# Weighted sums of latents for four heads at a time in the second attention of a hybrid layer stack

## The reference, cut to what matters

```
ckv, k_pe = split(x @ wkv_a)             # 64 latents, 64 rotary
ckv = rmsnorm(ckv) * kv_norm_scale       # [256, 64], shared by all heads
k_nope, v = split(ckv @ wkv_b)           # per head
attn = softmax(causal(q k^T * scale))    # per head [256, 256]
out = concat_h(attn_h @ v_h) @ wo
```

## Time and profile before

| | us |
|---|---|
| median of 3 runs (1255.74 to 1257.43) | 1257.11 |
| the profiled execution | 1257.83 |
| its span, first to last instruction | 1256.0 |
| TensorE matmul busy over the span | 1025.7 (82%) |
| VectorE busy | 802.9 (64%) |
| ScalarE busy | 555.0 (44%) |
| GpSimd busy | 170.1 (14%) |
| TensorE busy from 648 to 1064 | 383.3 of 416.0 |
| VectorE busy there | 258.1 |
| ScalarE busy there | 231.4 |
| mean granted clock of TensorE there | 0.98 of full |

### The profile page before, as it was taken

How to read it: one execution, slowest core, us unless ns; L and a number is a source line. 1 busy time by engine, 2 the same in 40 slices (tenths; PEclk the granted TensorE clock), 3 DMA queues, 4 the chain that set the end, 5 groups by cost and what they waited for, 6 DMA issues and landing times.

```text
span 1256.0 us, 21238 instructions
## 1 busy us (share of the span) xinstructions
PE 1025.7 (82%) x7024; PEld 779.9 (62%) x7024; DVE 802.9 (64%) x2776; ACT 555.0 (44%) x1561; POOL 170.1 (14%) x188
## 2 busy tenths in 40 slices
PE   0477777877875899992879898898989898799998
PEld 0465555655643677761757777676777776677774
DVE  3346776777674888860356665656666665688883
ACT  1135344544451254551135554546555465144445
POOL 4212211221100011000011111110111100001101
PEclk9888888988886999996699999999999999699999
DMA  4442234412402323225000000000000000333331
GB/s 168 73 74 50 45 55 74 73 32 45 74 2 41 74 57 74 59 43 206 1 1 1 1 1 1 1 1 1 1 1 1 2 1 1 72 74 75 82 82 31
DMA packets 55003, 55.01 MB, mean 44 GB/s; under 512 B 4960, under 2 KB 53616, under 8 KB 54768
## 3 DMA queue, kind: packets, MB, share of 16 engines
q1 hardware_dynamic: 54896, 53.66, 20.7%
HBM read 35.29 MB, written 17.83 MB: 42 GB/s over the span
## 4 chain that ended last, share of the span: by engine, by line
PE 68%; DVE 17%; issue 6%; POOL 3%; ACT 3%; DMA 2%; SPq 1%; POOLq 0%; DVEq 0%; ACTq 0%
PE bank L288 20%; PE bank L1263 6%; PE bank L367 5%; PE bank L1551 5%; PE bank L1406 4%; PE bank L1539 4%; PE bank L1420 3%; PE bank L1403 3%; PE bank L1592 2%; PE bank L1390 2%; PE bank L1441 2%; DVE arena L889 2%; PE bank L346 2%; DVE arena L1057 1%; PE bank L1260 1%
## 5 line engine op out<-in xcount | busy, mean ns | idle before, releaser
L675 ACT ACTIVATE arena<-arena,neg_max 128x153 f32<-128x153 f32 x256 | 94.0, 417 | 148.3 <-DVE arena L889 146.4
L1057 DVE TENSOR_REDUCE arena<-bank 128x2 f32<-128x512 f32 (+1 forms) x192 | 129.6, 682 | 30.2 <-PE bank L1406 29.4
L754 ACT ACTIVATE weights<-bank 128x512 f32<-128x512 f32 x144 | 85.8, 597 | 110.0 <-PE bank L1420 109.7
L680 ACT ACTIVATE weights<-bank,neg_max 128x128 f32<-128x128 f32 (+1 forms) x256 | 105.2, 419 | 47.9 <-DVE neg_max L892 47.8
L378 ACT ACTIVATE weights<-bank 128x384 f32<-128x384 f32 (+1 forms) x184 | 83.4, 453 | 68.6 <-PE bank L367 68.2
L1406 PE MATMUL bank<-kf_stack,q_stack 96*128 96x128 f32 (+1 forms) x512 | 111.0, 321 | 0.0
L1263 PE MATMUL bank<-kbT,arena 128*128 128x128 f32 (+1 forms) x512 | 107.1, 333 | 0.0
L346 PE MATMUL bank<-cst,xn 128*128 128x128 f32 x128 | 26.3, 342 | 96.6 <-DVE xn L337 94.6
L1420 PE MATMUL bank<-q_stack,kf_stack 98*128 98x512 f32 x192 | 97.8, 513 | 0.0
L901 DVE TENSOR_SCALAR weights<-weights,inv_sum 128x128 f32<-128x128 f32 (+1 forms) x256 | 84.9, 374 | 4.6
L892 DVE TENSOR_REDUCE neg_max<-bank 128x1 f32<-128x128 f32 (+1 forms) x256 | 78.6, 349 | 9.9 <-PE bank L1263 8.3
(11 more groups left out here) (217 smaller groups left out, 2650.3 us busy)
## 6 DMA issues: line engine op xcount, KB each, us to landing
q_stack<-scr_q SPq DMA_DIRECT2D x96, 128.0 KB, 3.8
scr_q<-q_hi SPq DMA_DIRECT2D x24, 256.0 KB, 2.4
scr_q<-q_lo SPq DMA_DIRECT2D x24, 256.0 KB, 2.5
q_stack<-scr_q SPq DMA_DIRECT2D x24, 256.0 KB, 6.3
ka_stack<-scr_k SPq DMA_DIRECT2D x24, 192.0 KB, 5.0
x_all<-x SPq DMA_DIRECT2D x8, 256.0 KB, 9.0
arena<-b_wqn SPq DMA_DIRECT2D x1, 2048.0 KB, 8.0
arena<-b_wo SPq DMA_DIRECT2D x1, 2048.0 KB, 16.9
```

Of the source, the lines that this page charges most:

```text
L675: last = a.activation(pg[:, g % 2, t, j, 0:KA], s_guard[:, h % 2, t, 0:KA], ACT.Exp, scale=-1.0, bias=neg_max[:, h % 4, t:t + 1])
L680: last = a.activation(probs[:, h % 4, t * P:t * P + n], ps_s[h % 2][:, t * P:t * P + n], ACT.Exp, bias=neg_max[:, h % 4, t:t + 1], accum_o ...
L1057: v.tensor_reduce(into, p1[k % 2][:, :].rearrange("p (h k) -> p h k", h=n), AX.X, ALU.max, negate=True).then_inc(s["maxed"], 1)
```

## The change

Four heads form a group. `attend_b` runs for group `g` at `h` = 4, 8, 12 and after head 15. One matmul takes two heads side by side in its moving operand (heads `4g + j` and `4g + j + 2`), so it has 512 columns for the first keys and 256 for the last; again 4 matmuls, now for four heads, and they fill both column halves of the bank. `act_ctx` copies 128 by 512 elements once per group into all of `oT`; it waits for the projections of the group before. `project_b` is as it was for each pair, but starts at `h` = 5 instead of 3, and the last two pairs are projected after the loop. ScalarE's `copy_probs` waits for groups instead of pairs before it overwrites slots of `probsT`.

```diff
-                        if h % 2 == 0 and h:
-                            attend_b(b, par, h // 2 - 1)
-                        if h % 2 == 1 and h > 2:
-                            project_b(b, (h - 3) // 2)
+                        if h % G == 0 and h:
+                            attend_b(b, par, h // G - 1)
+                        if h % 2 == 1 and h > G:
+                            project_b(b, (h - G) // 2)
...
-            def act_ctx(b, p):
+            def act_ctx(b, g):
-                act.wait_ge(*at(sm, "o_ps", b, p + 1))
-                act.wait_ge(*at(sm, "wo_ps", b, p - 1))
-                a.activation(oT[:, p % 2, :], halves(ps_o)[:, p % 2, :], ACT.Copy).then_inc(sm["oT"], 1)
+                act.wait_ge(*at(sm, "o_ps", b, g + 1))
+                act.wait_ge(*at(sm, "wo_ps", b, 2 * g))
+                a.activation(oT[:, :, :], halves(ps_o), ACT.Copy).then_inc(sm["oT"], 1)
...
-                        if h % 2 == 0 and h > 0:
-                            act_ctx(b, h // 2 - 1)
+                        if h % G == 0 and h > 0:
+                            act_ctx(b, h // G - 1)
...
-            def attend_b(b, par, p):
-                pe_wait_copies(sm, b, 2 * p, 2)
-                pe.wait_ge(*at(sm, "oT", b, p))
+            def attend_b(b, par, g):
+                pe_wait_copies(sm, b, G * g, G)
+                pe.wait_ge(*at(sm, "oT", b, g))
                 for k, (lo, n) in enumerate(((0, T), (T, P))):
                     for j in range(2):
-                        last = mm(halves(ps_o)[j * LORA:(j + 1) * LORA, p % 2, T - n:T], kv_tok[par][:, k, 0:LORA],
-                                  probsT[:, (2 * p + j) % 8, lo:lo + n], start=k == 0, stop=k == 1,
-                                  skip_group_check=True)
+                        h = G * g % 8 + j
+                        last = mm(halves(ps_o)[j * LORA:(j + 1) * LORA, :, T - n:T], kv_tok[par][:, k, 0:LORA],
+                                  probsT[:, h:h + 3:2, lo:lo + n], start=k == 0, stop=k == 1, skip_group_check=True)
...
-                pe.wait_ge(*at(sm, "oT", b, p + 1))
+                pe.wait_ge(*at(sm, "oT", b, p // 2 + 1))
...
-                attend_b(b, par, H // 2 - 1)
-                project_b(b, H // 2 - 1)
+                attend_b(b, par, H // G - 1)
+                for p in range(H // 2 - 2, H // 2):
+                    project_b(b, p)
```

More of the change, by code:

```diff
@@ L158, in signals @@
             if kind != "f":
-                n_act, n_out = len(ON_ACT[kind]), 2 * H // G if kind == "b" else H // G
+                n_act, n_out = len(ON_ACT[kind]), H // G
                 per |= dict(scores=H, maxed=H, exp=H, pT_ps=H, copy_dve=H - n_act, copy_act=n_act, oT=n_out, o_ps=n_out)
@@ L693, in heads @@
                         late = s["kind"] == "a" and h in YT_SLOTS and not first
-                        copy_probs(act, s, b, h, n, 2 if s["kind"] == "b" else G,
+                        copy_probs(act, s, b, h, n, G,
                                    (lambda half: act_yT(b - 1, YT_SLOTS.index(h), half)) if late else None)
                     if s["kind"] == "b":
-                        if h % 2 == 0 and h > 0:
-                            act_ctx(b, h // 2 - 1)
+                        if h % G == 0 and h > 0:
+                            act_ctx(b, h // G - 1)
                     else:
@@ L830, in batch_b @@
                 heads(sm, b, par, first, left, 3 * P, step_b)
-                act_ctx(b, H // 2 - 1)
+                act_ctx(b, H // G - 1)
             run_batches(act, lambda: start(sm, step_b), batch_b)
```

## The result

The changed kernel takes 1262.5 us (median of 19 runs) against 1257.7 in the 19 runs of the kernel before beside it: ratio 1.0035, 95% interval 1.0019 to 1.0051. By the ratio that is 4.4 us slower, between 2.4 and 6.4 (the two medians lie 4.8 apart). The forecast was no change, 1257.6, range 1252 to 1262. Its direction and its range were both missed, the range by half a microsecond.

The account below looks back on a forecast made before the run. TensorE bounds the inside of a batch, latency its edge. Seven batches +0.5, last batch +1.9, disturbed batches -1.9 sum to +0.5 us on 1257.8; that execution lies 0.7 above the median, so 1257.6, range 1252 to 1262.

Parts of the forecast that it names:

- head-by-head sum: Undisturbed batch of the second attention: gains inside the batch go back at its edge, +0.07 us per batch.
- the likeliest case: Whole kernel: no change, 1257.6 us, with its own range of 1255 to 1260; chance 0.55.
- The last batch: Final batch of the second attention, without preparation to fill TensorE: thinner cover, so +1.9 us.
- The term for the disturbed batches: Batches 2, 3 and 6, at half clock behind the edge: the attend removed at head 2 counts, -1.9 us.
- the gain at head 2: Disturbed batches, attend removed at head 2: 0.41 us to be had in batch 2, 1.0 taken for batch 3.
- TensorE is the bound everywhere: Every batch: saved fixed parts count in full, less the edge copy; -0.78 us per batch, 1251 us; chance 0.20.
- The halves don't overlap: Attend blocks: column halves don't overlap with 512 columns, 2.85 us instead of 1.55; 1290 us or more; chance 0.02.
- More half clock: Batch edges: longer waits bring half clock behind more edges, a fifth batch below clock 1; 1260.5 to 1263 us; chance 0.17.
- the hole: Head 2: with the attend block removed, TensorE gets a new wait of 0.9 us.
- the longer edge: Boundary between batches: attend, copy and one more projection lengthen the chain by 1.73 us, from 4.46 to 6.2.
- The Trainium skill's rule of about 60 cycles for each matmul: All attend blocks: 256 removed instructions worth 25 ns each, 6.4 us by estimate; the prediction held the trace against it.
- fixed: Attend block: time lost once on entry and exit beyond streaming, taken as 0.25 us for the new block too.

Follow-up runs that it names:

- The runs with one merging: Kernel before with one pair of pairs attended together: only pairs 0, 1 ratio 1.0013; 2, 3 0.9958; 4, 5 1.0012; 6, 7 1.0045.
- the two runs on it: Changed kernel with pair 0's sums made again, unread, after head 2: ratio 1.0032; changed kernel with pairs 6 and 7 attended separately: 0.9996.

## Why the prediction was wrong

**The head-by-head sum was right.** Per undisturbed batch I forecast +0.07; the traces give +0.08 to +0.1. Between the transposes of one head and the next, batch 1 of the two traces differs at heads 2, 3, 4, 6, 8, 10, 12, 14 and 15 by 0, -0.85, +0.63, -0.89, 0, -0.31, +0.64, -0.91, +1.72, with 0, -0.86, +0.65, -0.90, 0, -0.30, +0.65, -0.90, +1.73 forecast. The runs with one merging show that these are properties of the place. So the likeliest case was right in its mechanism.

**The last batch was somewhat mis-sized.** I forecast +1.9; the traces give +1.3. Heads 2 and 3 together gained 1.23 where I had 0.7, and from the transposes of head 15 to the last residual it took 1.44 more where I had 1.73.

**The term for the disturbed batches failed.** It read -1.9, from keeping the three stretches of half clock as they were and taking the removed attend out of them. The kernel after has three stretches again, but each is 6.8 us long instead of 3.4, 6.8 and 3.4. One costs 55.5 - 53.65 = 1.9 us, less than the 2.8 before, so the gain at head 2 is there (0.8, where I had 1.0). With the two longer stretches the three cost 5.8 us against 5.5: +0.3 in place of -1.9. My reason for leaving them alone was that nothing behind the residual addition changes. That held (the wait of 1.69 us there, below, is the same in both traces), and the stretches became longer all the same. With 0.6 from the seven batches and 1.3 from the last, the +0.3 makes 2.2 of the +2.3 of the second attention. What made two of the stretches longer isn't shown beyond where they begin (last section).

**One term wasn't in the sum at all.** I let the sum end with the layer and took the stages behind it for unchanged. The two traces have the second ffn 1.8 and 1.9 us longer. For the first, 2.3 + 1.8 = 4.1, against 4.4 measured; its whole span is only 3.6 longer because its second attention began 0.5 us earlier. That the ffn is longer in most runs of the change rests on the estimate at equal clock, and its cause is open.

**One wait was overlooked in the reading.** TensorE has a fourth gap per batch, the longest of all: 1.69 us at head 1, where the transposes of the normalized input wait for VectorE.

```profile
761.64 1.09 PE L346 MATMUL bank<-cst,xn 128*128 128x128 f32 x4 [1.69 <-DVE xn L337]
```

The change moves nothing there, so the sum doesn't suffer. But it is where the clock falls: the stretch of batch 2 begins at 761.04, inside this wait.

**The rivals.** "TensorE is the bound everywhere" fell: 53.6 us per batch, not 52.8. "The halves don't overlap" fell: 1.53 us per block. "More half clock" gave the sign, with 0.17, but not by its own mark: three edges were followed by half clock as before, the stretches behind them were longer, and neither the hole nor the longer edge alone makes them so, as the two runs on it show. The Trainium skill's rule of about 60 cycles for each matmul ("TensorEngine Tiling (Array Packing)", Instruction Overhead), read as a cost on top of the columns, would have made it 6.4 us faster, by estimate. The block for four heads, with the same 8 instructions and twice the columns, took 0.63 us more than the 0.90 of the block for two, with 0.24 fixed against 0.25, so it is the block and not the instruction that carries a cost.

The same page says that a change of tiling mode drains the engine (Key Properties). The trace agrees so far as that each such block loses 0.24 us beyond its streaming; it doesn't show which part is the drain.

## What to carry to other kernels

Write down, for each place where a block of work is taken away or added, which wait stands next behind it: the same merging was worth -0.9, +0.4, +0.6 or +0.65 us per batch, by the place alone. Where the bounding engine waits for a chain that the work to be moved doesn't belong to, move work into the wait (here a projection at head 9), and keep work out of the chain at the edge of a loop. For effects of 0.2%, compare stages of traces; medians of whole runs can differ by 2 us between two batches of runs of the same kernel.

## What the runs showed that I had not expected

The length of a stretch at half clock behind an edge goes by where it begins. In the 14 traces there are 36 such stretches in the second attention. The 22 that begin 1.91 to 2.26 us after the transposes of head 0 all last 6.8 us; the 14 that begin 2.36 to 4.51 us after them all last 3.4. That holds across kernels, with the hole at head 2 filled or open and with the edge short or long. Of the 36, 30 begin while TensorE waits for the normalized input at head 1 (1.69 us, in the two kernels with the residual later 1.93) and the other six at most 1.4 us after that wait. The wait is there in every whole batch, and most are followed by no half clock, so the wait alone doesn't bring it. These are observations; no run moved the beginning of a stretch by itself.

The stages behind a change can shift by as much as the change itself: the second ffn, the same code throughout, took 189.1 to 194.6 us in the 14 traces, with one to three stretches of half clock up to TensorE's last matmul.
